# A sandwich layer's opening: circulant tables loaded in quarters, and their product accumulated over eight PSUM banks

## The chip, the cores and the metric

One Trainium2 chip, all 8 cores. Each core runs the same program on one of the eight sequences of the batch; nothing is exchanged between cores. The metric is the device time of the slowest core, in microseconds.

## The reference

```python
# x: (8, 2048, 1024) float32; bind, unbind: (1024,); hidden 3072
def circ_conv(x, key): return irfft(rfft(x) * rfft(key), n=1024)
def circ_corr(x, key): return irfft(rfft(x) * conj(rfft(key)), n=1024)
def attn(x):
    bound = circ_conv(x, bind_key)
    d = sigmoid(decay)
    M = where(t >= s, d ** (t - s), 0)             # (T, T)
    hologram = einsum('ts,bsd->btd', M, bound)
    return x + gate * circ_corr(hologram, unbind_key)
def ffn(x):                                        # int weights / 127
    return (silu(x @ Wg.T) * (x @ Wu.T)) @ Wd.T
x = x + layernorm(attn(layernorm(x)))
x = x + layernorm(ffn(layernorm(x)))
```

Both circular operations are linear in x, so each is a 1024 x 1024 circulant matrix, and the two together are one matrix that does not depend on x. The kernel multiplies the two circulants first (the product is called hc) and applies hc after the decay.

## The kernel before

Each core holds its 2048 tokens as 16 tiles x of 128 tokens x 1024 features. The instructions of the five engines are written out in five lists; each engine runs its list in order, and `w(engine, semaphore, value)` puts a wait in front of the next instruction of that engine. `dma` adds a transfer to the list of SP (sync) or GpSimd (POOL), `op` an instruction. The stages, in order:

1. **Loads.** SP issues the 16 tiles of x, 512 KB each, in four groups with a semaphore each (LDX, LDX2, LDX3, LDX4; in the trace this is the hardware queue q1). GpSimd issues the constants, then cbtb and cubb, the two circulants, converted from float32 to bfloat16 on the way (the software queue q0). Each is a tile of 128 partitions x 8192 elements, one long row to a partition, and both count up one semaphore, WCC. Behind them GpSimd waits for all four groups of x and issues wdtb, the 6 MB of down weights, which are used from 450 us on.
2. **hc = cbtb x cubb** (line 236, called cp after its PSUM banks). There are 16 groups g of 128 x 512 outputs. A group accumulates over k = 0 to 7 into one of four banks, cp0 to cp3, and is then evicted by ScalarE (line 242, hc<-cp). From the fifth group on TensorE waits for the eviction of the group four before it.
3. **Statistics of the first layernorm** (lines 252 to 266, VectorE, bn_stats and bn_aggr), interleaved in the source with stage 2; every fourth tile waits for a group of x. `ln_combine` then makes scale and shift; its square root (line 283) is in ScalarE's list behind the 16 evictions. VectorE scales hc by the gate (line 305) and normalises x tile by tile into xw (line 315).
4. **Decay scan** (line 358, pb<-l0b,xw), four chunks of 512 tokens; **retrieval** with hc (line 475); layernorm and residual.
5. **FFN** in two halves of 1024 tokens: transposes (line 572), 24 steps of gate and up matmuls (lines 629, 637) whose weights wgu arrive two steps ahead on the software queue (512 KB each after conversion, 2048 elements to a partition), 8 tiles of down matmuls (line 706).

The lists hold every instruction in the order written; there is no scheduler. Stage 2 allocates four PSUM tiles of 128 x 512 float32, the scan behind it eight.

Of the kernel before, what the change touches and what calls it, by code (L numbers as in the profile page):

```python
# [8 lines left out]
F32 = mybir.dt.float32  # L9
BF16 = mybir.dt.bfloat16  # L10
I32 = mybir.dt.int32
AF = mybir.ActivationFunctionType
ALU = mybir.AluOpType

TN = 16
ND = 8
# [5 lines left out]
def build_nc(phases=99):  # L22
    nc = bass.Bass("TRN2", target_bir_lowering=False)

    xin = nc.dram_tensor("xin", [128, TN * 1024], F32, kind="ExternalInput")
    cbt = nc.dram_tensor("cbt", [128, ND * 1024], F32, kind="ExternalInput")
    cuT = nc.dram_tensor("cuT", [128, ND * 1024], F32, kind="ExternalInput")
# [5 lines left out]
    if phases < 90:  # L33
# [3 lines left out]
        st_o = nc.dram_tensor("st_o", [2, 128, 8], F32, kind="ExternalOutput")  # L37

    plan = {k: [] for k in ("sync", "gpsimd", "vector", "scalar", "tensor")}
    C = {"LDX": 0, "LDX2": 0, "LDX3": 0, "LDX4": 0, "LDC": 0, "WCC": 0, "WWD": 0,  # L40
         "WG0": 0, "WG1": 0, "PE": 0, "DV": 0, "SC": 0, "GP": 0, "ST": 0}
    S = {}

    def w(eng, sem, val):
        if val and val > 0:
            plan[eng].append(lambda e, s=sem, v=val: e.wait_ge(S[s], v))
# [3 lines left out]
    def gap(eng, cyc=300):  # L50
        n = max(1, cyc // 200)
        for _ in range(n):
            i = _gapn[eng] % 3
            _gapn[eng] += 1
            if eng == "vector":
                plan[eng].append(lambda e, i=i: e.tensor_copy(GAPT[:, i:i + 1], Z128[:]))
            else:
                plan[eng].append(lambda e, i=i: e.activation(GAPS[:, i:i + 1], Z128[:],
                                                             AF.Identity, bias=0.0, scale=1.0))

    def dma(eng, out_ap, in_ap, sem):
        C[sem] += 16
        plan[eng].append(lambda e, o=out_ap, i=in_ap, s=sem:
                         e.dma_start(out=o, in_=i).then_inc(S[s], 16))  # L64
        return C[sem]

    def op(eng, fn, sem=None):
        if sem is None:
            plan[eng].append(fn)
            return None  # L70
        C[sem] += 1
        plan[eng].append(lambda e, f=fn, s=sem: f(e).then_inc(S[s], 1))
        return C[sem]

    es = ExitStack()
    for name in C:
        S[name] = es.enter_context(nc.semaphore(name))
# [5 lines left out]
    HC = [sb(f"hc{j}", [128, 1024], BF16) for j in range(ND)]  # L83
# [27 lines left out]
    def aggr_out(MV, t):  # L111
        return MV[:, :].rearrange("p (two t) -> p two t", two=2)[:, :, t:t + 1]

    at = ExitStack()
# [8 lines left out]
    a2 = ExitStack()  # L123
    a2sb = lambda n, shp, dt: a2.enter_context(nc.sbuf_tensor(n, shp, dt))
    CBTB = a2sb("cbtb", [128, ND * 1024], BF16)
    CUBB = a2sb("cubb", [128, ND * 1024], BF16)
# [26 lines left out]
        dma("sync", X[t][:], xin[:, 1024 * t:1024 * t + 1024], f"LDX{t // 4 + 1}".replace("LDX1", "LDX"))  # L153
    ldx_tot = [4 * 16] * 4

    dma("gpsimd", CBTB[:], cbt[:, :], "WCC")
    wt_ccin = dma("gpsimd", CUBB[:], cuT[:, :], "WCC")
    for gname in ("LDX", "LDX2", "LDX3", "LDX4"):
        w("gpsimd", gname, 64)
    wt_wd = dma("gpsimd", WDTB[:], wdt[:, :], "WWD")  # L160
# [6 lines left out]
    def finish_debug(*inner_stacks, dump=()):  # L167
        w("sync", "DV", C["DV"])
        w("sync", "SC", C["SC"])
        w("sync", "PE", C["PE"])  # L170
        for snm in ("WCC", "WWD", "WG0", "WG1"):
            w("sync", snm, C[snm])
        for t in range(TN):
            dma("sync", out[t, :, :], X[t][:], "ST")
        for dst, tiles in dump:
            for i, tile in enumerate(tiles):
                dma("sync", dst[i, :, :], tile[:], "ST")
        w("sync", "ST", C["ST"])
        with nc.Block() as block:
            block.sync(lambda e: [f(e) for f in plan["sync"]] and None)  # L180
            block.gpsimd(lambda e: [f(e) for f in plan["gpsimd"]] and None)
            block.vector(lambda e: [f(e) for f in plan["vector"]] and None)
            block.scalar(lambda e: [f(e) for f in plan["scalar"]] and None)
            block.tensor(lambda e: [f(e) for f in plan["tensor"]] and None)
        for st in inner_stacks:
            st.close()
        es.close()
        return nc

    if phases <= 0.25:  # L190
# [5 lines left out]
                                                 bias=Z128[:], scale=1.0), "SC")  # L196
# [7 lines left out]
                                        bias=LNDc[0:1, :], scale=LNDc[0:1, :]))  # L204
    op("scalar", lambda e: e.activation(D512[:], E0M[0:1, 511:512], AF.Exp,
                                        bias=LNDc[0:1, :], scale=LNDc[0:1, :]))
    sc_lnd = 0
    for sg in range(4):
# [3 lines left out]
                                 bias=Z128[:], scale=LNDc[:]), "SC")  # L212
# [6 lines left out]
        return finish_debug(a2, at)  # L219

    pa = ExitStack()
    CP = [pa.enter_context(nc.psum_tensor(f"cp{i}", [128, 512], F32)) for i in range(4)]

    w("tensor", "WCC", wt_ccin)
    pe_cc = [0] * 16
    dv_ccevac = [0] * 16
    stat_fin = [0] * TN
    agg_fin = [0] * TN
    last_chain_end = {0: 0, 1: 0}
    for g in range(16):  # L230
        dj, fc = g // 2, g % 2
        if g >= 4:
            w("tensor", "SC", dv_ccevac[g - 4])
        for k in range(ND):
            pe_cc[g] = op("tensor", lambda e, dj=dj, fc=fc, k=k, g=g:
                          e.matmul(CP[g % 4][:], CBTB[:, 1024 * k + 128 * dj:1024 * k + 128 * dj + 128],  # L236
                                   CUBB[:, 1024 * k + 512 * fc:1024 * k + 512 * fc + 512],
                                   start=(k == 0), stop=(k == ND - 1)),
                          "PE" if k == ND - 1 else None)
        w("scalar", "PE", pe_cc[g])  # L240
        dv_ccevac[g] = op("scalar", lambda e, dj=dj, fc=fc, g=g:
                          e.activation(HC[dj][:, 512 * fc:512 * fc + 512], CP[g % 4][:],
                                       AF.Identity, bias=0.0, scale=1.0), "SC")
        if phases <= 0.77:
            continue
        t = g
        if t % 4 == 0:
            w("vector", f"LDX{t // 4 + 1}".replace("LDX1", "LDX"), 64)
        p = 12 * (t % 2)
        if t >= 2:  # L250
            w("vector", "DV", agg_fin[t - 2])
        op("vector", lambda e, t=t, p=p: e.bn_stats(STA[:, p:p + 6], X[t][:, 0:512]))
        stat_fin[t] = op("vector", lambda e, t=t, p=p: e.bn_stats(STA[:, p + 6:p + 12], X[t][:, 512:1024]), "DV")
        if t >= 1:
            q = 12 * ((t - 1) % 2)
            w("vector", "DV", stat_fin[t - 1])
            op("vector", lambda e, t=t, q=q: e.bn_aggr(aggr_out(MV1, t - 1), STA[:, q:q + 6]))
            gap("vector", 64)
            agg_fin[t - 1] = op("vector", lambda e, t=t, q=q: e.bn_aggr(aggr_out(MV2, t - 1), STA[:, q + 6:q + 12]), "DV")
# [3 lines left out]
    q = 12 * (15 % 2)  # L263
# [81 lines left out]
    for I in range(NCH):  # L345
# [3 lines left out]
        for d in range(ND):  # L349
            if I > 0:  # L350
# [3 lines left out]
                            start=True, stop=False, skip_group_check=True))  # L354
            for sg in range(4):
# [5 lines left out]
                                            start=(I == 0 and sg == 0), stop=(sg == 3),  # L361
# [7 lines left out]
        if I < NCH - 1:  # L369
            w("tensor", "SC", dv_ztevac[I][1])  # L370
            for dc in range(2):
                for sg in range(4):
# [3 lines left out]
                                           start=(sg == 0), stop=(sg == 3),  # L376
# [89 lines left out]
    for t in range(TN):  # L466
# [5 lines left out]
        for fc in range(2):  # L472
            for d in range(ND):
# [4 lines left out]
                            start=(d == 0), stop=False, skip_group_check=True))  # L478
# [3 lines left out]
                                     start=False, stop=True, skip_group_check=True), "PE")  # L482
# [105 lines left out]
    for hf in range(2):  # L588
# [27 lines left out]
        for eta in range(NH):  # L616
# [10 lines left out]
            for c in range(2):  # L627
                for d in range(ND):
# [4 lines left out]
                        start=(d == 0), stop=(d == ND - 1)),  # L633
                        "PE" if d == ND - 1 else None)
            for c in range(2):
                for d in range(ND):
# [4 lines left out]
                        start=(d == 0), stop=(d == ND - 1)),  # L641
# [57 lines left out]
        for tl in range(8):  # L699
            t = tg0 + tl  # L700
# [3 lines left out]
            for fc in range(2):  # L704
                for eta in range(NH):
# [4 lines left out]
                        start=(eta == 0), stop=(eta == NH - 1)),  # L710
# [92 lines left out]
```

## Time and profile before

| what | value |
|---|---|
| time, median of 2 runs | 818.92 us (818.87 to 818.97) |
| profiled execution, its own time | 819.88 us |
| its span, slowest core (core 7) | 818.3 us |
| spans of the 8 cores | 805.4 to 818.3 us |
| TensorE busy | 671.1 us, 82% of the span |
| VectorE, ScalarE busy | 248.8 us, 210.2 us |
| TensorE idle in front of its first matmul | 40.0 us |
| mean granted TensorE clock, core 7 | 0.910 |

The span runs from the first to the last instruction of the core; the time of an execution has about 1.6 us around it. Times within the profile are counted from the start of the span. Engines are PE (TensorE; PEld its weight loads), DVE (VectorE), ACT (ScalarE), POOL (GpSimd) and SP; "DMA share" is the mean busy share of the 16 DMA engines of the core. The granted clock is a share of 2.4 GHz.

### The profile page before, as it was taken

The numbers are of one execution on the slowest core, as the hardware profiler recorded it, in microseconds if no ns is written. First come the engines' busy times: TensorE is split into PE (matmuls) and PEld (weight loads), VectorE is DVE, ScalarE is ACT, GpSimd is POOL, SyncE is SP. The second block draws the span as 40 slices with busy tenths as digits, with TensorE's granted clock in tenths as the row PEclk, the third lists the DMA queues.
The fourth block names the chain that finished last, engine by engine and source line by source line (L and its number), as shares of the span: only waits on it lengthen the run. The fifth ranks groups of instructions, "written<-read, shape, count | busy, mean of one in ns | idle before, by whom it ended". The sixth has DMA issues, their size and how long they took to land.

```text
span 818.3 us, 8422 instructions; the slowest of 8 cores (805.4 to 818.3 us)
## 1 busy us (share of the span) xinstructions
PE 671.1 (82%) x3024; PEld 297.4 (36%) x3024; DVE 248.8 (30%) x595; ACT 210.2 (26%) x309; POOL 29.1 (4%) x58
## 2 busy tenths in 40 slices
PE   0095998997202899799999999598999999999993
PEld 0042322443102344344444444343444444444441
DVE  0276220455564226222222032223222222211233
ACT  2022422334424220311222122514112212213222
POOL 1000000000000000000000000000000000000000
PEclk9998655999755899899999999699999999999997
DMA  8989700000021144244444111014444444400111
GB/s 196 196 264 163 127 1 1 0 1 2 0 29 23 26 78 76 32 77 75 76 78 78 26 51 52 1 51 103 66 74 76 75 71 78 78 0 26 52 53 77
DMA packets 12281, 53.40 MB, mean 65 GB/s; under 512 B 1376, under 2 KB 1376, under 8 KB 11728
## 3 DMA queue, kind: packets, MB, share of 16 engines
q0 software_dynamic: 7632, 36.08, 26.2%
q1 hardware_dynamic: 4608, 16.78, 5.9%
q8 instruction: 25, 0.41, 0.2%
q14 instruction: 16, 0.13, 0.1%
HBM read 80.12 MB, written 8.39 MB: 108 GB/s over the span
## 4 chain that ended last, share of the span: by engine, by line
PE 74%; DVE 9%; issue 6%; ACT 5%; DMA 4%; DVEq 0%; POOL 0%; ACTq 0%; POOLq 0%
PE pg L629 20%; PE pu L637 19%; PE pu L706 10%; PE pf L706 10%; DMA cubb<-cuT 4%; PE pb L358 4%; PE cp L236 4%; ACT t1a L433 2%; DVE sqd L412 2%; PE pt L572 2%; ACT t1a L405 2%; PE pb L353 1%; DVE sta L537 1%; DVE x2t L576 1%; PE pr L475 1%
## 5 line engine op out<-in xcount | busy, mean ns | idle before, releaser
L629 PE MATMUL pg<-x2t,wgu 128*128 128x512 bf16 x768 | 177.3, 385 | 11.6 <-DVE xw L656 8.0
L637 PE MATMUL pu<-x2t,wgu 128*128 128x512 bf16 x768 | 173.6, 379 | 0.0
L650 ACT ACTIVATE sil<-pg,z 128x512 bf16<-128x512 f32 x96 | 65.6, 689 | 243.0 <-PE pg L629 242.9
L629 PEld LDWEIGHTS pg<-x2t,wgu 128*128 128x128 bf16 x768 | 75.1, 99 | 107.7 <-issue 22.5
L637 PEld LDWEIGHTS pu<-x2t,wgu 128*128 128x128 bf16 x768 | 75.1, 98 | 90.6
L656 DVE SCALAR_TENSOR_TENSOR xw<-sil,pu 128x512 bf16<-128x512 bf16 x64 | 43.7, 688 | 169.0 <-PE pu L637 166.9
L475 PE MATMUL pr<-hc,zt 128*128 128x512 bf16 x256 | 62.1, 387 | 7.6 <-ACT t1a L405 6.6
L236 PE MATMUL cp<-cubb,cbtb 128*128 128x512 bf16 x128 | 31.3, 412 | 40.0 <-DMA cubb<-cuT 40.0
L572 PE MATMUL pt<-idb_s,x2s 128*128 128x128 bf16 x128 | 15.8, 300 | 58.7 <-ACT x2s L562 45.5
L706 PE MATMUL pu<-wdtb,xw 128*128 128x512 bf16 x256 | 60.0, 389 | 0.0
L706 PE MATMUL pf<-wdtb,xw 128*128 128x512 bf16 x256 | 57.9, 379 | 2.2 <-DVE hc L656 2.2
L656 DVE SCALAR_TENSOR_TENSOR hc<-sil,pu 128x512 bf16<-128x512 bf16 x32 | 22.0, 688 | 89.5 <-PE pu L637 89.5
L64 POOL DMA_DIRECT2D wgu<-wgu x48 | 25.4, 529 | 624.5 <-PE pu L637 444.4
L437 DVE TENSOR_TENSOR x<-x,t1f 128x1024 f32<-128x1024 f32 x16 | 19.6, 1225 | 82.4 <-ACT t1f L433 82.4
L358 PE MATMUL pb<-l0b,xw 128*128 128x512 bf16 (+3 forms) x128 | 35.4, 437 | 9.3 <-DVE xw L315 9.3
L475 PEld LDWEIGHTS pr<-hc,zt 128*128 128x128 bf16 x256 | 25.0, 99 | 40.3 <-issue 12.5
L706 PEld LDWEIGHTS pu<-wdtb,xw 128*128 128x128 bf16 x256 | 25.6, 100 | 31.6 <-issue 2.8
L706 PEld LDWEIGHTS pf<-wdtb,xw 128*128 128x128 bf16 x256 | 24.9, 98 | 32.9 <-issue 3.1
L572 PEld LDWEIGHTS pt<-idb_s,x2s 128*128 128x128 bf16 x128 | 12.0, 134 | 62.9 <-issue 62.9
L236 PEld LDWEIGHTS cp<-cubb,cbtb 128*128 128x128 bf16 x128 | 13.2, 104 | 57.5 <-issue 46.2
L422 ACT ACTIVATE scr<-scr,epsc 128x1 f32<-128x1 f32 x32 | 9.5, 297 | 92.7 <-DVE scr L418 86.4
L706 PE MATMUL pf<-wdtb,hc 128*128 128x512 bf16 x128 | 30.2, 379 | 0.0
(91 smaller groups left out, 441.3 us busy)
## 6 DMA issues: line engine op xcount, KB each, us to landing
wgu<-wgu POOLq DMA_DIRECT2D x48, 512.0 KB, 5.2
x<-xin SPq DMA_DIRECT2D x16, 512.0 KB, 36.4
out<-x SPq DMA_DIRECT2D x16, 512.0 KB, 2.6
wdtb<-wdt POOLq DMA_DIRECT2D x1, 6144.0 KB, 41.2
cbtb<-cbt POOLq DMA_DIRECT2D x1, 2048.0 KB, 22.1
cubb<-cuT POOLq DMA_DIRECT2D x1, 2048.0 KB, 36.0
cstf_s<-cstf POOLq DMA_DIRECT2D x1, 257.0 KB, 8.3
cstb_s<-cstb POOLq DMA_DIRECT2D x1, 128.0 KB, 8.5
```

The source lines that it names most:

```text
L64: e.dma_start(out=o, in_=i).then_inc(S[s], 16))
L236: e.matmul(CP[g % 4][:], CBTB[:, 1024 * k + 128 * dj:1024 * k + 128 * dj + 128], CUBB[:, 1024 * k + 512 * fc:1024 * k + 512 * fc + 512], s ...
L358: e.matmul(PB[d][:, 128 * sg:512], XW[4 * I + sg][:, 128 * d:128 * d + 128], L0B[:, 0:512 - 128 * sg], start=(I == 0 and sg == 0), stop=(s ...
L405: return op("scalar", lambda e: e.activation(Tb[:], PSRC[:], AF.Identity, bias=0.0, scale=1.0, accum_out=SCR[:, c:c + 1]), "SC")
L437: dv_xadd = op("vector", lambda e: e.tensor_tensor(Xt[:], Xt[:], Tb[:], ALU.add), "DV")
L475: e.matmul(PR[p][:, 512 * fc:512 * fc + 512], ZT[d][:, 128 * t:128 * t + 128], HC[d][:, 512 * fc:512 * fc + 512], start=(d == 0), stop=Fal ...
L572: pe_tr[tl] = op("tensor", lambda e, tl=tl, d=d: e.transpose(PT[:, 128 * d:128 * d + 128], X2S[tl % 2][:, 128 * d:128 * d + 128], IDB[:]), ...
L629: pe_g[eta][c] = op("tensor", lambda e, sl=sl, c=c, d=d: e.matmul(PG[sl][:, 512 * c:512 * c + 512], WGU[sl][:, 128 * d:128 * d + 128], X2T ...
L637: pe_u[eta][c] = op("tensor", lambda e, sl=sl, c=c, d=d: e.matmul(PU[sl][:, 512 * c:512 * c + 512], WGU[sl][:, 1024 + 128 * d:1024 + 128 * ...
L650: sc_sil[eta][c] = op("scalar", lambda e, sl=sl, c=c: e.activation(SIL[sl][:, 512 * c:512 * c + 512], PG[sl][:, 512 * c:512 * c + 512], AF ...
L656: dv_ht[eta][c] = op("vector", lambda e, eta=eta, sl=sl, c=c: e.scalar_tensor_tensor(HT(eta)[:, 512 * c:512 * c + 512], SIL[sl][:, 512 * c ...
L706: pe_dn[tl] = op("tensor", lambda e, sl=sl, tl=tl, fc=fc, eta=eta: e.matmul(PFS[sl][:, 512 * fc:512 * fc + 512], HT(eta)[:, 128 * tl:128 * ...
```

## The change

Each of the two circulant tables is loaded in four transfers of 2048 columns instead of one of 8192. Quarter q holds k = 2q and 2q + 1 of all groups; the quarters of the two tables alternate on GpSimd's queue, and the two transfers of a quarter share a semaphore, WK0 to WK3. The product uses eight PSUM banks. The sixteen groups are worked in two halves of eight; in a half, k is the outer loop and the group the inner one, so that all eight banks accumulate side by side and close one after the other with k = 7. In the first half TensorE waits for each quarter as it comes to it; in front of the second half it waits for the eighth eviction. The evictions stand in ScalarE's list eight behind each half. The statistics loop is written behind the product instead of in it; it has the same instructions for VectorE in the same order.

```diff
--- before.py
+++ after.py
@@ -37,7 +37,8 @@
         st_o = nc.dram_tensor("st_o", [2, 128, 8], F32, kind="ExternalOutput")
 
     plan = {k: [] for k in ("sync", "gpsimd", "vector", "scalar", "tensor")}
-    C = {"LDX": 0, "LDX2": 0, "LDX3": 0, "LDX4": 0, "LDC": 0, "WCC": 0, "WWD": 0,
+    C = {"LDX": 0, "LDX2": 0, "LDX3": 0, "LDX4": 0, "LDC": 0,
+         "WK0": 0, "WK1": 0, "WK2": 0, "WK3": 0, "WWD": 0,
          "WG0": 0, "WG1": 0, "PE": 0, "DV": 0, "SC": 0, "GP": 0, "ST": 0}
     S = {}
 
@@ -153,8 +154,9 @@
         dma("sync", X[t][:], xin[:, 1024 * t:1024 * t + 1024], f"LDX{t // 4 + 1}".replace("LDX1", "LDX"))
     ldx_tot = [4 * 16] * 4
 
-    dma("gpsimd", CBTB[:], cbt[:, :], "WCC")
-    wt_ccin = dma("gpsimd", CUBB[:], cuT[:, :], "WCC")
+    for q in range(4):
+        dma("gpsimd", CBTB[:, 2048 * q:2048 * q + 2048], cbt[:, 2048 * q:2048 * q + 2048], f"WK{q}")
+        dma("gpsimd", CUBB[:, 2048 * q:2048 * q + 2048], cuT[:, 2048 * q:2048 * q + 2048], f"WK{q}")
     for gname in ("LDX", "LDX2", "LDX3", "LDX4"):
         w("gpsimd", gname, 64)
     wt_wd = dma("gpsimd", WDTB[:], wdt[:, :], "WWD")
@@ -219,31 +221,37 @@
         return finish_debug(a2, at)
 
     pa = ExitStack()
-    CP = [pa.enter_context(nc.psum_tensor(f"cp{i}", [128, 512], F32)) for i in range(4)]
-
-    w("tensor", "WCC", wt_ccin)
+    CP = [pa.enter_context(nc.psum_tensor(f"cp{i}", [128, 512], F32)) for i in range(8)]
+
     pe_cc = [0] * 16
     dv_ccevac = [0] * 16
     stat_fin = [0] * TN
     agg_fin = [0] * TN
     last_chain_end = {0: 0, 1: 0}
-    for g in range(16):
-        dj, fc = g // 2, g % 2
-        if g >= 4:
-            w("tensor", "SC", dv_ccevac[g - 4])
+    for half in range(2):
+        g0 = 8 * half
+        if half == 1:
+            w("tensor", "SC", dv_ccevac[7])
         for k in range(ND):
-            pe_cc[g] = op("tensor", lambda e, dj=dj, fc=fc, k=k, g=g:
-                          e.matmul(CP[g % 4][:], CBTB[:, 1024 * k + 128 * dj:1024 * k + 128 * dj + 128],
-                                   CUBB[:, 1024 * k + 512 * fc:1024 * k + 512 * fc + 512],
-                                   start=(k == 0), stop=(k == ND - 1)),
-                          "PE" if k == ND - 1 else None)
-        w("scalar", "PE", pe_cc[g])
-        dv_ccevac[g] = op("scalar", lambda e, dj=dj, fc=fc, g=g:
-                          e.activation(HC[dj][:, 512 * fc:512 * fc + 512], CP[g % 4][:],
-                                       AF.Identity, bias=0.0, scale=1.0), "SC")
-        if phases <= 0.77:
-            continue
-        t = g
+            if half == 0:
+                w("tensor", f"WK{k // 2}", 32)
+            for g in range(g0, g0 + 8):
+                dj, fc = g // 2, g % 2
+                pe_cc[g] = op("tensor", lambda e, dj=dj, fc=fc, k=k, g=g:
+                              e.matmul(CP[g % 8][:],
+                                       CBTB[:, 1024 * k + 128 * dj:1024 * k + 128 * dj + 128],
+                                       CUBB[:, 1024 * k + 512 * fc:1024 * k + 512 * fc + 512],
+                                       start=(k == 0), stop=(k == ND - 1)),
+                              "PE" if k == ND - 1 else None)
+        for g in range(g0, g0 + 8):
+            dj, fc = g // 2, g % 2
+            w("scalar", "PE", pe_cc[g])
+            dv_ccevac[g] = op("scalar", lambda e, dj=dj, fc=fc, g=g:
+                              e.activation(HC[dj][:, 512 * fc:512 * fc + 512], CP[g % 8][:],
+                                           AF.Identity, bias=0.0, scale=1.0), "SC")
+    if phases <= 0.77:
+        return finish_debug(pa, a2, at)
+    for t in range(TN):
         if t % 4 == 0:
             w("vector", f"LDX{t // 4 + 1}".replace("LDX1", "LDX"), 64)
         p = 12 * (t % 2)
```

On TensorE at the start of the list, with the waits (names in brackets are semaphores; SC counts ScalarE's instructions), before:

```order
1 L236 MATMUL cp<-cubb,cbtb 128x512 [waits WCC]
2 L236 MATMUL cp<-cubb,cbtb 128x512 x31
3 L236 MATMUL cp<-cubb,cbtb 128x512 [waits SC]
4 L236 MATMUL cp<-cubb,cbtb 128x512 x7
5 L236 MATMUL cp<-cubb,cbtb 128x512 [waits SC]
```

and with the change:

```order
9 L241 MATMUL cp<-cubb,cbtb 128x512 [waits WK2]
10 L241 MATMUL cp<-cubb,cbtb 128x512 x7
11 L241 MATMUL cp<-cubb,cbtb 128x512 [waits WK2]
12 L241 MATMUL cp<-cubb,cbtb 128x512 x7
13 L241 MATMUL cp<-cubb,cbtb 128x512 [waits WK3]
14 L241 MATMUL cp<-cubb,cbtb 128x512 x7
15 L241 MATMUL cp<-cubb,cbtb 128x512 [waits WK3]
16 L241 MATMUL cp<-cubb,cbtb 128x512 x7
17 L241 MATMUL cp<-cubb,cbtb 128x512 [waits SC]
18 L241 MATMUL cp<-cubb,cbtb 128x512 x63
```

Before, one wait for the tables stands in front of all, and twelve waits for an eviction are spread over the last twelve groups. With the change the waits for the tables are spread over the first 64 matmuls, and one wait for evictions is left, in front of the last 64.

On GpSimd's queue, behind the constants, before:

```order
8 L64 DMA cbtb<-cbt 128x8192
9 L64 DMA cubb<-cuT 128x8192
10 L64 DMA wdtb<-wdt 128x2x12288 [waits LDX,LDX2,LDX3,LDX4]
11 L64 DMA wgu<-wgu 128x2048 [waits PE,DV,SC]
```

and with the change:

```order
8 L65 DMA cbtb<-cbt 128x2048
9 L65 DMA cubb<-cuT 128x2048
10 L65 DMA cbtb<-cbt 128x2048
11 L65 DMA cubb<-cuT 128x2048
12 L65 DMA cbtb<-cbt 128x2048
13 L65 DMA cubb<-cuT 128x2048
14 L65 DMA cbtb<-cbt 128x2048
15 L65 DMA cubb<-cuT 128x2048
16 L65 DMA wdtb<-wdt 128x2x12288 [waits LDX,LDX2,LDX3,LDX4]
```

Two transfers became eight, of a quarter of the row length each.

## Rows read from the trace of the kernel before

**Rows 1.** Chain of waits, 0 to 95 us: start us, us, what.

```profile
3.83 36.02 DMA cubb<-cuT
...
39.99 31.30 PE cp L236 x128
...
71.99 1.28 ACT L283
...
80.56 7.34 PE pb L358 x32
```

**Rows 2.** Timeline, 0 to 90 us: start us, us, engine, line, instruction [idle before it <-releaser].

```profile
3.31 0.56 POOL L64 DMA_DIRECT2D cbtb<-cbt  x1
...
25.67 0.69 DVE L252 BATCH_NORM_STATS2 sta<-x 128x6 f32<-128x512 f32 x1 [6.80 <-DMA x<-xin]
...
43.66 0.60 ACT L242 ACTIVATE hc<-cp 128x512 bf16<-128x512 f32 x1 [25.40 <-PE cp L236]
...
46.37 0.60 ACT L242 ACTIVATE hc<-cp 128x512 bf16<-128x512 f32 x1 [2.11 <-PE cp L236]
...
48.09 0.60 ACT L242 ACTIVATE hc<-cp 128x512 bf16<-128x512 f32 x1 [1.13 <-PE cp L236]
...
58.37 0.71 POOL L64 DMA_DIRECT2D wdtb<-wdt  x1 [53.96 <-DMA x<-xin]
...
66.26 0.17 DVE L280 SCALAR_TENSOR_TENSOR ws<-ws 128x16 f32<-128x16 f32 x1
...
71.37 0.60 ACT L242 ACTIVATE hc<-cp 128x512 bf16<-128x512 f32 x1 [1.13 <-PE cp L236]
...
86.91 1.69 ACT L382 ACTIVATE zt<-pb 128x512 bf16<-128x512 f32 x3 [0.17 <-PE pb L358]
```

**Rows 3.** Windows: stretch, length, busy us and count by engine; PEclk, DMA share, GB/s.

```profile
40.00:45.00 5.00, 5.00 (x12) 1.72 (x13) 0.00 (x0) 0.60 (x1) 0.00 (x0) 1.00 0.98 315
...
50.00:55.00 5.00, 5.00 (x23) 2.21 (x22) 4.16 (x15) 1.61 (x3) 0.00 (x0) 0.94 0.99 323
55.00:60.00 5.00, 5.00 (x22) 2.19 (x21) 4.69 (x17) 1.79 (x3) 0.71 (x1) 0.88 0.55 143
...
80.00:85.00 5.00, 4.44 (x17) 2.33 (x18) 3.31 (x5) 1.79 (x3) 0.00 (x0) 0.50 0.98 172
85.00:90.00 5.00, 4.72 (x24) 2.08 (x22) 0.09 (x1) 2.88 (x5) 0.00 (x0) 0.86 1.00 159
```

**Rows 4.** DMA queues, 12 to 36 us: packets, MB, share of 16 engines.

```profile
q0 software_dynamic: 230, 3.51, 86.3%
q1 hardware_dynamic: 229, 0.87, 13.7%
```

**Rows 5.** DMA queues, 9 to 11 us.

```profile
q0 software_dynamic: 96, 0.35, 74.7%
q1 hardware_dynamic: 89, 0.31, 46.5%
```

**Rows 6.** DMA, 40 to 45 us, x alone: all packets by size, and the queue.

```profile
DMA packets 432, 1.57 MB, mean 315 GB/s; under 512 B 48, under 2 KB 48, under 8 KB 432
...
q1 hardware_dynamic: 432, 1.57, 98.2%
```

**Rows 7.** DMA queues, 300 to 400 us, 13 transfers of wgu.

```profile
q0 software_dynamic: 1872, 6.82, 40.0%
```

**Rows 8.** DMA queue of x, 0 to 5 us, and 5 to 9 us.

```profile
q1 hardware_dynamic: 161, 0.61, 46.1%
...
q1 hardware_dynamic: 177, 0.64, 74.0%
```

**Rows 9.** DMA issues of the page: count, KB each, us to landing.

```profile
wgu<-wgu POOLq DMA_DIRECT2D x48, 512.0 KB, 5.2
```

**Rows 10.** Timeline of TensorE, 320 to 340 us, and 505 to 556 us.

```profile
334.56 5.77 PE L629 MATMUL pg<-x2t,wgu 128*128 128x512 bf16 x16 [5.47 <-DVE xw L656]
...
553.80 2.53 PE L629 MATMUL pg<-x2t,wgu 128*128 128x512 bf16 x11 [1.63 <-ACT t1f L405]
```

## The prediction

> **What bounds the kernel now.** I read the chain that ended last first, then the timeline of the opening, then the queues that fill it, then the clock. The chain says that TensorE's work sets the end almost everywhere, but that the first 40 us of the span belong to a transfer: cubb, issued at 3.83, takes 36.02 us, and only then do the 128 cp matmuls run, for 31.3 us [rows 1]. Behind them the chain goes through ScalarE and VectorE: the last eviction of cp ends at 71.97, then come an activation table, the square root of the first layernorm, the scaling of hc and the normalising of four x tiles, and the first pb matmul starts at 80.56, 8.6 us after the last eviction [rows 1, 2]. The layernorm statistics are no rival of that chain: the last input of the square root starts at 66.26 and is done at 66.43, so the square root stands queued on ScalarE behind the evictions for 5.5 us [rows 2]. So the time of the change is read from one number: when the sixteenth eviction of cp ends. Everything behind follows it, one for one.
>
> **What the change removes.** Wait for the whole of cbtb and cubb goes; TensorE may start with a quarter of each. Of the 128 matmuls, 48 (k = 0 to 5 of the first eight groups) can be done while the last quarter is still on its way. At the fast pace a matmul takes 0.216 us (8 matmuls between evictions at 46.37 and 48.09), at the slow one, at which the stage starts, 0.427 (12 starts in the 5 us from 40; the first eviction at 43.66 is 39.99 plus 8 such plus 0.25) [rows 1 to 3]. If the last quarter landed when cubb lands today, at 39.86, this would take 48 matmuls off the path behind it.
>
> **What it adds at the evictions.** Before, ScalarE drained a group while TensorE worked on the next three. Now all eight banks close together, so eight evictions stand in a row twice. Back to back an eviction of this shape costs 1.69 / 3 = 0.563 us [rows 2], eight cost 4.5 us. Let L be the landing of the last quarter. Sixteen matmuls are then left of the first half. TensorE has had pauses, and I take them at the slow pace: the ninth closes group 0 at L + 3.8, ScalarE starts at L + 4.1 and has drained the eighth bank at L + 8.7. TensorE's second half waits for that one, though a bank is free at L + 4.7. Then 64 matmuls at 0.216: group 8 closes with the 57th, 12.3 us later, at L + 21.0; the evictions run from L + 21.25 to L + 25.8. Before, the same moment was 71.97 - 39.86 = 32.1 us behind the landing. So the reorder is worth 6.3 us less what L moves.
>
> **What it does to the transfers.** This is where I expect it to lose. The bytes are the same, and all 16 engines of the DMA are full in this stretch, 86.3% and 13.7% of the time for the two queues, and 98.2% for x alone once cubb is in [rows 4, 6]. The question is who gets them. While cbtb and cubb load, the software queue moved 230 packets and the hardware queue, with x, 229 [rows 4]: they take turns, one packet each, though a packet of the software queue carried 3.51 MB / 230 = 15.3 KB on average, one row of 16 KB but for the few that only count the semaphore, and one of x 4 KB. So the long row is what buys cbtb and cubb their share. Between 9 and 11 us, when the software queue carries the constants in packets of about 4 KB, the turns are 96 to 89 [rows 5]: they go by packets at that size too. The change cuts each row of 8192 elements into four of 2048, which is the shape of wgu. So 256 packets become 1024 of 4 KB, and x gets a turn between any two.
>
> The Trainium skill's page "DMA: Bandwidth & Descriptors", section "Queues, rings and completion order", says the same of the arbiter, that each engine goes round robin between its queues packet by packet; its typical 9 to 17 descriptors to a packet the trace does not show, where a row of cbtb is a packet of its own. By the rule in its typical form the cut would still shrink the share.
>
> The prices, per engine: a packet of cbtb now 24 x 16 x 0.863 / 230 = 1.44 us, x beside it 24 x 16 x 0.137 / 229 = 0.23; x alone 5 x 16 x 0.982 / 384 = 0.205 (432 packets less 48 that only count the semaphore); a 4 KB packet of wgu 100 x 16 x 0.400 / 1664 = 0.385 (13 transfers of 128 rows) [rows 4, 6, 7]. Check on before: both transfers have 16 rows an engine, 16 x (1.44 + 0.23) = 26.7 us from about 11.0, so 37.7; cubb landed at 39.86, 2.1 later, which I keep as the lag of the slowest engine. After: 64 x (0.385 + 0.205) = 37.8, so 48.8, plus 2.1: L = 50.9. With x at 0.23, L = 52.5. From the other end: x moved 0.61 + 0.64 + 0.31 = 1.56 MB before 11 us [rows 5, 8], 24 packets an engine; 64 more go beside cubb, so 40 are left behind it, 8.2 us; as the bytes are the same x still ends at 57 to 58, so L = 49.3, or 47.2 if the slowest engine's lag is in that end already. The bounds are 47.2 and 52.5, and I take 51.0, nearest to the sum that reproduces before.
>
> So the last eviction ends at 51.0 + 25.8 = 76.8 against 71.97: **4.8 us later**. The quarters land about 9.5 us apart (16 pairs of 0.59), from 20 on; the first 48 matmuls hide between them at either pace (16 x 0.427 = 6.8 us).
>
> **Edits at nothing.** Six more issues on GpSimd's queue cost some 0.56 us each, in front of a wait for x that ends at 58.37 [rows 2]: covered, and the eighth is issued at about 7.5, while the constants still load. x's first groups come earlier; VectorE's statistics still end with the fourth group, now at 66.43, and after within a microsecond or two of it, some 10 us ahead of the new last eviction; should x end later than that, they would be the bound. The load of wdtb waits for x's landing, which does not move, and has until 450 us. If that cover were gone, each would cost its own length.
>
> **The sum.** The profiled execution took 819.9 us with a span of 818.3; plus 4.8 it is 824.7. The median of the runs shown lies 1.0 below it, so I forecast 823.7.
>
> **The rivals.**
> *The turns do not go against the chunks.* Had the software queue kept its 86%, L would stay at about 40 and the evictions would end at 65.7. Then the statistics take over as the bound, at 66.43: 5.5 us gained, 813.4. For it: the even turns are measured with long rows and, at 4 KB, only over 2 us. Against it: both rows agree to 8%. 0.15.
> *The clock falls in the broken stretches.* TensorE pauses between quarters and again about 2 us for the evictions. After the 9.3 us pause ending at 80.56 the granted clock was 0.50 (1.2 GHz of 2.4), and 0.86 on average over the next 5 us; after 5.5 us ending at 334.56, 16 matmuls took 5.77 instead of 3.6; after one of 1.6 us at 553.8 nothing was lost [rows 3, 10]. If the second half starts slow too, its first 5.4 us do 12.7 matmuls instead of 25, 2.7 us: 826.4, and with the dearer L of 52.5, 828. 0.17. If, the other way, the last sixteen run fast, 1.8 us less, 821.9, inside the forecast.
> *Each transfer costs its fixed part in series.* One wgu took 5.2 us from issue to landing [rows 9] where its eight packets an engine cost 3.1, so 2.1 are fixed; six more in series would be 12.7 us, and the end 17.5 later at 836.4, slower by 2.1%. Against it: x's transfers of the same 512 KB follow each other with the engines 98.2% busy [rows 6]. The same page of the Trainium skill has this rule, 2.0 us and a part by size for each transfer, and advice to batch from 1 MiB; the row of x speaks against its holding for queued transfers. 0.03, and it decides only if a queue lets its transfers in one by one.
>
> **How the numbers follow.** The forecast case holds 0.65, from 47.2 to 52.5 for L: +1.0 to +6.3, 819.9 to 825.2. The dip of the clock under load, 0.94 and 0.88 in the ten microseconds from 50 [rows 3], costs 0.9 us before and may cost 1 more after. The other sign takes 0.15 and reaches to 813.4; most of it (a part of the share kept) lies over 815. Above, 829 takes in the slow start, the dear L and the dip. So 815 to 829. Two per cent, 16.4 us, about what a measurement of this kernel tells from no change, is out of reach of all but the serial rival: faster 0.01, within 0.97, slower 0.02.
>
> **What would show it.** In the profile after: cubb's last landing near 51; while it loads, equal packet counts of the two queues but about 65% of the time for the software one; x's first statistics before 20 us instead of 25.67; cp matmuls from about 20, in bursts of 16; a pause of TensorE of some 2 us in front of the last 64; two rows of eight evictions; the first pb matmul at about 85.4. I am wrong if the last quarter lands near 40 (turns), or if the second half takes well over 14 us (clock).

## The result and the profile after

The changed kernel takes 824.14 us (median of 13 runs) against 818.62 us (median of 12): ratio 1.0069, 95% interval 1.0046 to 1.0093. That is 0.7% slower, clear of noise and within 2%. In some executions of several kernels here, the kernel before among them, the cores of one or both dies run at a lower granted clock and the time is longer (903.43 and 914.15 us among the 13 of the changed kernel, 816.79 and 823.59 among the four of the kernel "x held, scan's pauses filled" below): the medians count them, the ratios and intervals leave them out. The profiled execution took 823.54 us with a span of 822.0 on core 2, against 819.88 and 818.3 for the kernel before.

The chain of waits of the changed kernel over its first 90 us (start us, us, what) answers to [rows 1]:

```profile
6.96 45.44 DMA cubb<-cuT
...
57.94 2.11 ACT hc L250 x4
...
60.19 7.71 PE cp L241 x35
67.95 6.22 PE cp L241 x28
...
74.67 2.10 ACT hc L250 x4
76.79 1.28 ACT L291
...
85.36 5.34 PE pb L366 x24
```

The last quarter lands at 6.96 + 45.44 = 52.4 us, where the whole tables had landed at 39.86. Evictions (hc) now stand on the chain twice, once between the halves of the product and once behind it. The activation table behind the last eviction is loaded at 76.79 instead of 71.99, and the first pb matmul starts at 85.36 instead of 80.56: 4.8 us later on both counts.

The DMA queues of the changed kernel from 12 to 48 us (packets, MB, share of the 16 engines) answer to [rows 4]:

```profile
q0 software_dynamic: 1035, 3.78, 64.0%
q1 hardware_dynamic: 1039, 3.80, 37.9%
```

The counts are as equal as before (230 and 229), but a packet of the tables now carries 4 KB and not 16 KB. Their share of the engines fell from 86.3% to 64.0%. (The two shares add up to 101.9%: the recorded times of packets overlap a little.)

The timeline of TensorE (start us, us, instruction, [idle before <-releaser]):

```profile
22.41 6.29 PE L241 MATMUL cp<-cubb,cbtb 128*128 128x512 bf16 x16 [22.41 <-DMA cubb<-cuT]
33.27 5.98 PE L241 MATMUL cp<-cubb,cbtb 128*128 128x512 bf16 x16 [4.57 <-DMA cubb<-cuT]
43.65 5.92 PE L241 MATMUL cp<-cubb,cbtb 128*128 128x512 bf16 x16 [4.39 <-DMA cubb<-cuT]
52.53 0.59 PE L241 MATMUL cp<-cubb,cbtb 128*128 128x512 bf16 x1 [2.97 <-DMA cubb<-cuT]
53.34 4.09 PE L241 MATMUL cp<-cubb,cbtb 128*128 128x512 bf16 x14 [0.22 <-issue]
60.19 13.97 PE L241 MATMUL cp<-cubb,cbtb 128*128 128x512 bf16 x63 [2.76 <-ACT hc L250]
85.36 6.43 PE L366 MATMUL pb<-l0b,xw 128*128 128x512 bf16 x31 [11.20 <-DVE xw L323]
```

Three bursts of 16 hide between the landings; the fourth starts at the last one, then TensorE pauses 2.76 us for the eighth eviction, and the second half runs at full pace (13.97 us). The other engines, to compare with [rows 2]:

```profile
19.36 0.69 DVE L260 BATCH_NORM_STATS2 sta<-x 128x6 f32<-128x512 f32 x1
...
56.02 4.03 ACT L250 ACTIVATE hc<-cp 128x512 bf16<-128x512 f32 x8 [37.18 <-PE cp L241]
...
60.40 0.71 POOL L65 DMA_DIRECT2D wdtb<-wdt  x1 [52.81 <-DMA x<-xin]
...
68.46 0.18 DVE L288 SCALAR_TENSOR_TENSOR ws<-ws 128x16 f32<-128x16 f32 x1
```

x's first group is in by 19.4 instead of 25.67. Its last group ends at 60.4 instead of 58.37, and the statistics at 68.6 instead of 66.4, still 8 us ahead of the end of the last eviction. Eight evictions in a row take 4.03 us.

### The profile page after: what moved, and what is told of

The parts are those of the page before. It is cut to its first block, busy times and chain, and to the rows that moved or that the text cites. A ratio compares the mean times of both kernels' runs of the same rounds, so it can differ in the third digit from the quotient of the medians.

```text
span 822.0 us, 8366 instructions; the slowest of 8 cores (809.4 to 822.0 us)
## 1 busy us (share of the span) xinstructions
PE 672.8 (82%) x2966; PEld 299.1 (36%) x3024; DVE 248.5 (30%) x595; ACT 208.3 (25%) x309; POOL 32.3 (4%) x64
## 4 chain that ended last, share of the span: by engine, by line
PE 71%; DVE 9%; issue 7%; DMA 6%; ACT 6%; POOL 1%; DVEq 0%; ACTq 0%; POOLq 0%
PE pg L637 20%; PE pu L645 19%; PE pu L714 10%; PE pf L714 10%; DMA cubb<-cuT 6%; PE pb L366 4%; PE cp L241 2%; ACT t1a L441 2%; DVE sqd L420 2%; PE pt L580 2%; ACT t1a L413 2%; PE pb L361 1%; DVE sta L545 1%; DVE x2t L584 1%; PE pr L483 1%
## 5 line engine op out<-in xcount | busy, mean ns | idle before, releaser
L637 PEld LDWEIGHTS pg<-x2t,wgu 128*128 128x128 bf16 x768 | 75.8, 99 | 106.1 <-issue 20.2
L241 PE MATMUL cp<-cubb,cbtb 128*128 128x512 bf16 x126 | 36.8, 459 | 37.4 <-DMA cubb<-cuT 34.3
L580 PE MATMUL pt<-idb_s,x2s 128*128 128x128 bf16 x128 | 16.2, 306 | 58.7 <-ACT x2s L570 45.5
L714 PE MATMUL pu<-wdtb,xw 128*128 128x512 bf16 x251 | 58.1, 383 | 0.4 <-issue 0.2
L445 DVE TENSOR_TENSOR x<-x,t1f 128x1024 f32<-128x1024 f32 x16 | 19.6, 1225 | 81.4 <-ACT t1f L441 81.4
L366 PE MATMUL pb<-l0b,xw 128*128 128x384 bf16 (+3 forms) x125 | 34.3, 431 | 11.7 <-DVE xw L323 11.2
L580 PEld LDWEIGHTS pt<-idb_s,x2s 128*128 128x128 bf16 x128 | 12.4, 137 | 63.0 <-issue 63.0
L714 PE MATMUL pu<-wdtb,hc 128*128 128x512 bf16 x126 | 30.0, 379 | 0.1
## 6 DMA issues: line engine op xcount, KB each, us to landing
wdtb<-wdt POOLq DMA_DIRECT2D x1, 6144.0 KB, 40.6
```

Of the source, the lines that this page charges most:

```text
L241: e.matmul(CP[g % 8][:], CBTB[:, 1024 * k + 128 * dj:1024 * k + 128 * dj + 128], CUBB[:, 1024 * k + 512 * fc:1024 * k + 512 * fc + 512], s ...
L366: e.matmul(PB[d][:, 128 * sg:512], XW[4 * I + sg][:, 128 * d:128 * d + 128], L0B[:, 0:512 - 128 * sg], start=(I == 0 and sg == 0), stop=(s ...
L445: dv_xadd = op("vector", lambda e: e.tensor_tensor(Xt[:], Xt[:], Tb[:], ALU.add), "DV")
L580: pe_tr[tl] = op("tensor", lambda e, tl=tl, d=d: e.transpose(PT[:, 128 * d:128 * d + 128], X2S[tl % 2][:, 128 * d:128 * d + 128], IDB[:]), ...
L637: pe_g[eta][c] = op("tensor", lambda e, sl=sl, c=c, d=d: e.matmul(PG[sl][:, 512 * c:512 * c + 512], WGU[sl][:, 128 * d:128 * d + 128], X2T ...
L714: pe_dn[tl] = op("tensor", lambda e, sl=sl, tl=tl, fc=fc, eta=eta: e.matmul(PFS[sl][:, 512 * fc:512 * fc + 512], HT(eta)[:, 128 * tl:128 * ...
```

## The experiments

Each kernel is timed against the kernel before on the same chip, and its profile gives the moments, in us, on its slowest core. "Last landing" is when the last piece of the two tables is in, "eviction" the end of the last eviction of cp, "scan" the start of the first pb matmul.

| kernel | last landing | eviction | scan | ratio to before, 95% interval |
|---|---|---|---|---|
| before | 39.9 | 72.0 | 80.6 | 1 |
| changed | 52.4 | 76.8 | 85.4 | 1.0069 [1.0046, 1.0093] |
| loads only | 53.3 | 84.4 | 93.0 | 1.0145 [1.0126, 1.0164] |
| order only | 40.5 | 78.1 | 86.7 | 1.0085 [1.0065, 1.0104] |
| halves | 43.4 | 74.5 | 83.1 | 1.0073 [1.0049, 1.0097] |
| second half by group | 52.9 | 72.9 | 81.4 | 1.0001 [0.9985, 1.0017] |
| x held | 40.1 | 64.7 | 75.2 | 0.9929 [0.9911, 0.9948] |
| x held, second half by group | 39.6 | 60.5 | 75.0 | 0.9954 [0.9936, 0.9971] |
| x cut | 42.7 | 67.4 | 76.0 | 0.9962 [0.9948, 0.9975] |
| x held, scan's pauses filled | 40.5 | 67.2 | 75.8 | 0.9715 [0.9694, 0.9736] |
| the same, pause in front filled too | 39.9 | 66.6 | 76.2 | 0.9696 [0.9679, 0.9713] |

**The loads alone.** The product stays in the order of the kernel before and waits for all eight pieces.

```diff
-    dma("gpsimd", CBTB[:], cbt[:, :], "WCC")
-    wt_ccin = dma("gpsimd", CUBB[:], cuT[:, :], "WCC")
+    for q in range(4):
+        dma("gpsimd", CBTB[:, 2048 * q:2048 * q + 2048], cbt[:, 2048 * q:2048 * q + 2048], f"WK{q}")
+        dma("gpsimd", CUBB[:, 2048 * q:2048 * q + 2048], cuT[:, 2048 * q:2048 * q + 2048], f"WK{q}")
-    w("tensor", "WCC", wt_ccin)
+    for q in range(4):
+        w("tensor", f"WK{q}", 32)
```

> Theory (the queues take turns by packet, so short rows lose share to x): the last of the eight pieces lands at 51 to 52 us instead of 39.9, the product, in the old order, still starts only then, and its last eviction ends 32.1 us later, at 83 to 84: about 11.5 us slower than the kernel before, 830. Rival (the split is harmless and the new order of the product costs the time): last landing near 40, time as before, 818.6.

Its chain of waits:

```profile
6.96 46.37 DMA cubb<-cuT
...
84.44 1.28 ACT L285
```

The landing is at 53.3, 13.5 us late, the eviction 12.4 us late, and the ratio is 1.45%, 11.8 us. The split on its own costs that much, and the rival (a harmless split) is out.

**The order alone.** The changed kernel with the two whole transfers.

```diff
-    for q in range(4):
-        dma("gpsimd", CBTB[:, 2048 * q:2048 * q + 2048], cbt[:, 2048 * q:2048 * q + 2048], f"WK{q}")
-        dma("gpsimd", CUBB[:, 2048 * q:2048 * q + 2048], cuT[:, 2048 * q:2048 * q + 2048], f"WK{q}")
+    dma("gpsimd", CBTB[:], cbt[:, :], "WK0")
+    dma("gpsimd", CUBB[:], cuT[:, :], "WK0")
```

TensorE waits for WK0 once, in front of k = 0 (not shown).

> Theory: with whole rows the tables land at 39.9 as before; but now all 128 matmuls lie behind that, plus a pause of some 3 us in front of the second half and a tail of eight evictions, so the last eviction ends near 76.8 instead of 72: 4.8 us slower than before, 823.4. Rival (the order costs nothing, all comes from the transfers): 818.6.

TensorE's timeline:

```profile
40.58 16.67 PE L240 MATMUL cp<-cubb,cbtb 128*128 128x512 bf16 x64 [40.58 <-DMA cubb<-cuT]
60.01 15.50 PE L240 MATMUL cp<-cubb,cbtb 128*128 128x512 bf16 x64 [2.76 <-ACT hc L249]
86.71 5.62 PE L365 MATMUL pb<-l0b,xw 128*128 128x512 bf16 x26 [11.20 <-DVE xw L322]
```

The first half takes 16.67 us, the pause is 2.76, and the last eviction ends at 78.1. That is 1.3 us later than expected: the landing is 0.6 later than in the kernel before, and the second half takes 15.50 us on this core where the changed kernel took 13.97, because it starts slow (the granted clock is 0.61 on average from 60 to 64 us and 1.00 behind that); the evictions, 4.03 us for eight instead of 4.5, give part of it back. So each part of the change costs time on its own, 11.8 and 7.0 us by the ratios. Together they cost 5.6, because only together do 48 matmuls fit in front of the last landing.

**Halves.** Two pieces of 4096 columns instead of four, the first waited for at k = 0 and the second at k = 4.

> Theory: rows of 4096 elements are packets of 8 KB, 32 turns an engine at about 0.74 + 0.205 us, so the last piece lands at 43 to 44; 32 matmuls are left behind it instead of 16, the last eviction ends near 73: 1 to 2 us slower than before, 820. Rival (turns do not go by packet, but the time goes with the pause and the tail alone): landing near 40 and the last eviction near 70, 816.5.

Its queues from 12 to 36 us:

```profile
q0 software_dynamic: 428, 3.11, 76.8%
q1 hardware_dynamic: 429, 1.56, 23.7%
```

Packets of 8 KB, again turn by turn, and a share between the two others: 86.3%, 76.8%, 64% for 16, 8 and 4 KB. The landing is the expected one, 43.4. The last eviction ends at 74.5 where 73 was expected, the scan starts 2.5 us later than before, and the ratio is 0.73%, 6 us where 1 to 2 were forecast. The windows of this kernel's slowest core, core 1, and of core 5 on the other die show what was added (the number behind the POOL column is the granted clock):

```profile
145.00:200.00 55.00, 54.66 (x202) 22.38 (x203) 25.30 (x66) 20.75 (x35) 0.00 (x0) 0.79 0.00 1
...
145.00:200.00 55.00, 52.30 (x231) 22.75 (x229) 26.91 (x71) 21.39 (x36) 0.00 (x0) 0.96 0.00 1
```

The same stretch of the kernel before, core 7, ran at 1.00. Here all four cores of die 0 are at 0.79 to 0.81 in it, and none of die 1 is below 0.96. The low clock is there in the other stages of die 0 as well: on core 1 the second half of the product takes 16.96 us instead of 13.97, the scan 62.2 instead of the 60.1 of the kernel before, and the matmuls of the retrieval 75.8 instead of 71.6, of which later stages make up a part. Core 5, the slowest of die 1, has a span of 819.7 us, 1.4 us above that of the kernel before: the 1 to 2 us of the forecast. The times agree: of the four executions, three have two to four cores with a mean clock of 0.88 or 0.89 and take 823.7 to 825.7 us, and the one that has none takes 820.65, where 820 was forecast. So most of the excess over the forecast goes with the lower clock of one die and not with the size of the pieces. Why that die's clock was lower no run tells.

**The second half group by group.** In the second half of the changed kernel k is the inner loop again, each group waits for its own bank alone and is evicted as it closes. (`cc_mm` issues one matmul and `cc_evac` one eviction, both as in the changed kernel; the first half is written with them too.)

```diff
+    for g in range(8, 16):
+        w("tensor", "SC", dv_ccevac[g - 8])
+        for k in range(ND):
+            cc_mm(g, k)
+        cc_evac(g)
```

> Theory: the landing stays near 51 to 52, the pause of 2.8 us in front of the second half goes (group 8 needs only bank 0), and so does the tail, since evictions follow every 1.73 us: the last eviction ends 4.5 us earlier than in the changed kernel, 72.2, and the time is that of the kernel before, 819.5. Rival (pause and tail were covered by something else, such as the statistics): no gain on the changed kernel, 824.

TensorE's timeline:

```profile
53.06 19.11 PE L234 MATMUL cp<-cubb,cbtb 128*128 128x512 bf16 x78 [4.07 <-DMA cubb<-cuT]
81.45 5.99 PE L372 MATMUL pb<-l0b,xw 128*128 128x512 bf16 x31 [9.28 <-DVE xw L329]
```

The last 80 matmuls (two records are missing) run without a pause, and the last eviction ends at 72.9, 3.9 us sooner although the landing is 0.5 later. The ratio is 1.0001. The pause and the tail are thus the whole 0.7% of the change; without them the late landing is paid by the matmuls that were done ahead of it, within the 0.2% of the interval.

**x held.** The changed kernel; SP issues four tiles of x, then waits for the third quarter.

```diff
     for t in range(TN):
+        if t == 4:
+            w("sync", "WK2", 32)
         dma("sync", X[t][:], ...)
```

> The changed kernel, with SP waiting for the third quarter before it issues x tiles 4 to 15. Theory (turns by packet): with x's four first tiles gone the software queue has the engines to itself, 40 packets an engine at 0.385 instead of 0.59; the last quarter lands near 42.6 instead of 51, the last eviction ends near 68, x ends near 60 and the statistics near 68.5, which become the bound together: 4 us faster than before, 815. Rival (each transfer costs a fixed part, whatever else is queued): the last quarter still lands near 51 and x later, 824 or more.

The queues from 12 to 36 us, and the chain:

```profile
q0 software_dynamic: 1043, 3.81, 98.2%
q1 hardware_dynamic: 100, 0.34, 5.3%
```

```profile
37.99 14.32 DMA x<-xin
...
66.62 1.28 ACT L293
```

The same eight transfers with the same short rows land at 40.1 once x is out of the way: 12 us earlier than in the changed kernel, and 2.5 earlier than expected. It was x's turns, not the number of transfers: a fixed part for each transfer in series would have left the landing where it was, and with the tables' packets busy for 98.2% of the engines' time there is no room for one. The evictions end at 64.7, the square root's table is loaded only at 66.62, behind the statistics, and x is now on the chain. The ratio is 0.71% below the kernel before, 5.8 us where 4 were forecast.

**x held, and the second half group by group.** Both edits together.

> As the one with x held, and the second half of the product group by group. Theory: the product is done near 64 and no longer the bound; the statistics behind the last x tile are, near 68.5, so the time is the same as with x held alone or up to 1 us less, 814 to 815. Rival (the product's pause and tail still bound): 4.5 us less than with x held alone.

The product is done at 60.5 and the scan starts at 75.0, against 75.2. The intervals of the two ratios (0.9911 to 0.9948, 0.9936 to 0.9971) overlap, so no gain is shown, and certainly not the 4.5 us of the rival. Where the statistics bound, the pause and the tail of the evictions cost nothing, as the theory said.

**x cut.** The changed kernel with each x tile in two transfers of 512 columns.

```diff
-        dma("sync", X[t][:], xin[:, 1024 * t:1024 * t + 1024], ...)
+        for h in range(2):
+            dma("sync", X[t][:, 512 * h:512 * h + 512], xin[:, 1024 * t + 512 * h:1024 * t + 512 * h + 512], ...)
```

(The waits for a group of x count twice as many increments; not shown.)

> The changed kernel, with each x tile loaded in two transfers of 512 columns, 2 KB rows. Theory (a turn is a packet, and a packet a row): x's turns carry half as much, the packet counts of the two queues stay equal, and the last quarter lands earlier, at 45 to 48 instead of 51, at the price of x: 820 to 822. Rival (a turn is a fixed amount of bytes or time, short rows being joined): equal bytes to a turn as in the changed kernel, landing near 51, 824.

Its queues from 12 to 36 us:

```profile
q0 software_dynamic: 864, 3.15, 76.2%
q1 hardware_dynamic: 862, 1.57, 26.1%
```

Equal counts again, with 1.57 MB in 862 packets: x's packets are 2 KB rows, but for the 96 that only count a semaphore. Per engine a turn of x with data costs 24 x 16 x 0.261 / 766 = 0.13 us, where it is 0.235 beside the tables in the changed kernel (worked out below), and the tables land at 42.7 instead of 52.4, below the 45 to 48 expected. The time beats the kernel before by 0.4%, 3.1 us, where a loss of 1.4 to 3.4 us had been expected (820 to 822).

**The scan's pauses filled.** The stage behind the change had shown a spread that I could not pass over. From the first pb matmul to the first pr matmul the cores took 51.6 to 60.1 us in the kernel before, seven of the eight about 60, and 45.5 to 62.2 over all kernels so far. What differs is the granted clock. Here are the scan of the slowest core of the kernel before, and that of the fastest core of the kernel with x held (stretch, length, PE busy and count, granted clock, DMA share, GB/s):

```profile
80.56:140.60 60.04, 53.64 (x176) 0.61 0.29 46
...
74.00:119.60 45.60, 39.12 (x176) 0.86 0.47 78
```

As many matmuls, and a mean clock of 0.61 against 0.86. TensorE pauses 1.84 us between the scan's chunks, for the state that VectorE updates. With x held, each of the three pauses was filled:

```diff
         if I < NCH - 1:
+            w("tensor", "SC", dv_ztevac[I][2])
+            for _ in range(8):
+                op("tensor", lambda e: e.matmul(PB[2][:, 0:512], IDBT[:], L0B[:, 0:512],
+                                                start=True, stop=True, skip_group_check=True))
```

The added wait is for the eviction of the bank that the idle matmuls write.

> The kernel with x held, with eight idle matmuls of 128x512 into a free PSUM bank in each of the three pauses of TensorE between the chunks of the decay scan; their results are overwritten. The scan took between 45.6 and 62.2 us on the cores of the kernels so far, and the slowest core nearly always 60. Theory A (the pause lets the granted clock fall to a half, and the slow clock is what the long scans are made of): the scan of the slowest core falls to 46 to 54 us, 5 to 12 us less than with x held alone, 803 to 808. Theory B (the clock falls because the scan's own one-row and one-column matmuls are too thin, whatever stands in the pause): the granted clock still falls to a half behind the filling, the scan stays at 60 and the filling adds up to 2 us a pause: 813 to 818.

TensorE's timeline, a window of it and the window of the whole scan (busy, granted clock, DMA share, GB/s):

```profile
82.41 1.89 PE L384 MATMUL pb<-xw,wcb 128*1 128x512 bf16 x8
84.23 1.90 PE L397 MATMUL pb<-l0b,idb_s 128*128 128x512 bf16 x8
86.13 0.37 PE L363 MATMUL pb<-dpb,srowb 1*128 1x512 bf16 x1
```

```profile
90.00:95.00 5.00, 5.00 (x27) 1.00 0.97 162
...
75.80:117.80 42.00, 40.98 (x200) 0.95 0.55 94
```

The filling ends where the wait did, the granted clock is 1.00 behind it and 0.95 over the scan, and the stage takes 41.2 to 42.8 us on all eight cores. The ratio to the kernel before is 0.9715, 2.2% below x held alone; it rests on two of four executions, 795.43 us (the profiled one) and 793.61. Theory A had put the stage at 46 to 54 us and so underrated the filling; theory B fell, since the thin matmuls are all still there. The filling was tried only on top of x held, not on the kernel before.

**The pause in front filled too.**

```diff
+    for _ in range(44):
+        op("tensor", lambda e: e.matmul(PB[2][:, 0:512], IDBT[:], L0B[:, 0:512],
+                                        start=True, stop=True, skip_group_check=True))
```

> As the one before, with 44 more idle matmuls in the pause of 13 us in front of the scan. Theory A: the scan also starts at full clock, the first 32 matmuls take 4.5 instead of 6 to 7.4 us: 1.5 to 3 us less than with the three pauses filled. Theory B: the first chunk is 1.5 to 3 us faster and the rest at 60 as before. Either: if the idle matmuls load the chip so that the clock dips to 0.81, part of this is given back.

```profile
66.69 9.66 PE L346 MATMUL pb<-l0b,idb_s 128*128 128x512 bf16 x43 [2.76 <-ACT hc L252]
76.19 4.51 PE L371 MATMUL pb<-l0b,xw 128*128 128x512 bf16 x31
```

793.13 us, ratio 0.9696, the lowest of all. The first chunk takes the 4.5 us that theory A gave it, 2.2 less than the 6.69 of the kernel with the three pauses filled. But 44 matmuls are too many: they run for 9.66 us, and the scan starts 9.6 us behind the last eviction (66.6 to 76.2) instead of the 8.6 of the kernels in which the evictions bind, so that about 1 us is given back. The two intervals (0.9694 to 0.9736, 0.9679 to 0.9713) overlap, and a gain in the time is not shown.

## Why the prediction was right, step by step

*The bound.* The end of the sixteenth eviction governed: it moved 4.8 us, and the first pb matmul 4.8 us. In most experiments the ratio followed the start of the first pb matmul within 2 us: 12.4 us for the loads alone gave 11.8, 6.1 for the order alone 7.0, 0.9 for the second half by group 0.1, -5.4 for x held -5.8, -5.6 for both -3.8, -4.6 for x cut -3.1. The halves are the exception, 2.5 against 6.0, with the lower clock of one die in three of their four executions.

*What x takes.* Turn for turn by packet held in four stages with different sizes of packet, and this was the step on which the sign hung. The counts were 1035 to 1039 where 230 to 229 had been measured, and the share of the software queue 64.0% where 65% was forecast. The landing was at 52.4, inside the bounds but later than my 51.0, and the term that was too small is the price of a pair of packets. For wgu and for x alone I had taken out the packets that only count a semaphore; for cbtb I had divided by all 230. All packets in the stretches of [rows 4] and of its counterpart, before and after:

```profile
DMA packets 459, 4.38 MB, mean 182 GB/s; under 512 B 32, under 2 KB 32, under 8 KB 245
...
DMA packets 2075, 7.59 MB, mean 211 GB/s; under 512 B 224, under 2 KB 224, under 8 KB 2074
```

Before, 32 of the 459 packets are small ones, 16 on each queue, which leaves 214 of the tables and 213 of x: 24 x 16 x 0.863 / 214 = 1.55 us and 24 x 16 x 0.137 / 213 = 0.25, and sixteen such pairs from 11.0 end at 39.7. The landing was at 39.86: the lag of 2.1 us, which I gave to a slowest engine and carried over, is almost nothing but this divisor. After, 224 are small, 112 on each queue, which leaves 923 (3.78 MB in rows of 4 KB) and 927: 36 x 16 x 0.640 / 923 = 0.399 us and 36 x 16 x 0.379 / 927 = 0.235, a pair 0.634 where I had 0.59. Sixty-four pairs are 40.6 us, 51.6 on the clock, 0.8 before the landing. So x beside the tables kept its dearer price of 0.23, as in my upper bound of 52.5, and a 4 KB packet of the tables cost 0.399 instead of 0.385. The first quarter shows the same: it was in at 22.4 and not at 20, and the others followed 10.0 us apart on average instead of 9.5. The check from the other end had failed in the same term: x did not end at 57 to 58 "as the bytes are the same" but at 60.4, and 8.2 us in front of that is 52.2. That my point lay within 1.4 us of the landing is in part luck: the cheap pair took 2.8 us from the sum and the false lag gave 1.3 of them back.

*The evictions.* The shape was right, and the pause was 2.76 us where "some 2" stood. The term was too large by 1.4: the eviction ended 24.4 us behind the landing instead of 25.8. Eight evictions took 4.03 us instead of 4.5, twice, which is 0.9 of it. The rest is mostly that ScalarE started 3.6 us behind the landing instead of 4.1. The whole fourth burst took 4.9 us (52.53 to 57.43) instead of 6.8, because the clock rose in it, but only its first nine matmuls stand in front of the first eviction. This error and the late landing cancelled, so that 76.8 was hit closer than its terms deserve.

*The sum.* Plus 5.5 us between the medians against plus 4.8 forecast; 824.1 against 823.7. The agreement to 0.4 us owes something to that cancelling; the direction and the two mechanisms do not.

*The rivals.* The turns did go against the chunks. The fixed cost of each transfer in series did not come: with x held, the packets of the eight transfers took 98.2% of the engines' time from 12 to 36 us, and the last landed at 40.1. The Trainium skill, page "DMA: Bandwidth & Descriptors", section "Anatomy of one DMA — SWDGE (gpsimd) path", gives 2.0 us and a part by size for one DMA; for transfers that stand in a queue behind each other, the trace just named shows that the fixed part was not paid one after the other. The clock rival did not come in the second half on the slowest core (13.97 us), but it did on others: cores 3 and 6 took 15.6 and 15.4, and core 6 ended at 821.9, level with the slowest. So it cost the time of this kernel next to nothing, while in the kernel with the order alone it cost the slowest core 1.5. Its larger place was the scan, which the prediction had left out: there a pause of 1.84 us, shorter than the 2 us I had worried about, went with it.

## What to carry to other kernels

Before a load is cut to start work sooner, look at what shares the DMA engines with it: here two queues took turns packet by packet, and cutting rows from 16 to 4 KB gave 38% of the engines instead of 14% to data that was not wanted first. Hold the other queue, or cut its rows instead. When an accumulation is turned inside out to follow a load, turn it back for the part that no longer waits: banks that close together must be drained together, twice 4 us here. When a price is read from a count of packets, take out those that only count a semaphore, in every row alike. And look at the spread of one stage over the cores; a stage that takes 46 us on one core and 60 on the slowest is worth more than what was being tuned.

## What the runs showed of the hardware

- The turns of the two queues went by packet, whatever the packets held: 16, 8 and 4 KB on the software queue against 4 KB on the hardware queue, and 4 KB against 2 KB, in these four in equal numbers within 1% (230 to 229, 428 to 429, 1035 to 1039, 864 to 862).
- A packet of 4 KB of x took 0.235 us of an engine beside the tables and 0.205 alone; a packet of the tables 1.55 us for 16 KB and 0.399 for 4 KB. Those that only count a semaphore (16 for each transfer) took about 0.01 us.
- Eight transfers of 512 KB on the software queue, with the other queue held back, followed each other with the engines 98.2% busy and landed at 40.1 us; two of 2 MB beside the other queue landed at 39.9.
- The 1.84 us pauses between the chunks of the scan, each behind eight matmuls of one column, went with a granted clock of half speed over most of the next chunk; eight full matmuls in each pause raised the mean over the scan from 0.61 to 0.95 and took the stage from 60 us on the slowest core to 42. Why other cores took 46, 52 or 54 us with the same pauses no run shows.
- All four cores of one die of the kernel with halves ran at 0.79 to 0.81 of full clock for 55 us while TensorE was busy 98% of the time or more; in the kernel before, the slowest core dipped for a few microseconds only (0.94 and 0.88, [rows 3]).
